# State-space scan on one core: transposed drive in blocks of 64 steps, B diagonals by state group, delta copied inside SBUF

## The reference

```
u: (B, K=4, D_INNER=192, L=4096)        four scan directions
x_dbl = einsum('bkdl,kcd->bkcl', u, x_proj_weight)
dts, Bs, Cs = split(x_dbl, [6, 6 + 16], axis=2)
delta = softplus(einsum('bkrl,kdr->bkdl', dts, dt_projs_weight) + dt_projs_bias)
A = -exp(A_logs)                        # (K, 192, 16)
for t in range(L):                      # h: (B, K, 192, 16)
    h = h * exp(delta_t[..., None] * A) + (delta_t * u_t)[..., None] * B_t[:, :, None, :]
    y_t = einsum('bkdn,bkn->bkd', h, C_t)
```

## Time and profile before

| what | us |
|---|---|
| median of 3 runs (16163.91 to 16176.15) | 16174.73 |
| the profiled execution, its own time | 16179.37 |
| span of that execution in the trace | 16176.9 |
| PE busy, share of the span | 12939.1, 80% |
| DVE busy | 9552.7, 59% |
| POOL busy | 8899.6, 55% |
| ACT busy | 7503.2, 46% |

### The profile page before, as it was taken

How to read it: one execution, slowest core, us unless ns; L and a number is a source line. 1 busy time by engine, 2 the same in 40 slices (tenths; PEclk the granted TensorE clock), 3 DMA queues, 4 the chain that set the end, 5 groups by cost and what they waited for, 6 DMA issues and landing times.

```text
span 16176.9 us, 551693 instructions
## 1 busy us (share of the span) xinstructions
PE 12939.1 (80%) x223648; PEld 6772.7 (42%) x223648; DVE 9552.7 (59%) x14966; ACT 7503.2 (46%) x14253; POOL 8899.6 (55%) x4341
## 2 busy tenths in 40 slices
PE   7888778887788877888778887788877888778887
PEld 3444434444344443444434444344443444434444
DVE  4666446664466644666446674466744667346673
ACT  4544344443444434445344453444534445344553
POOL 3666336663366633666346672466624667246672
PEclk9999699996899968999699996999969999699996
DMA  3444124441244412444124441344413444134441
GB/s 86 109 109 111 34 71 109 111 108 34 73 107 110 108 35 72 109 111 108 33 76 110 105 110 32 77 108 106 110 33 77 108 105 111 32 78 106 107 110 28
DMA packets 1044001, 1404.93 MB, mean 87 GB/s; under 512 B 461935, under 2 KB 463504, under 8 KB 1041148
## 3 DMA queue, kind: packets, MB, share of 16 engines
q1 hardware_dynamic: 1041660, 1369.95, 33.3%
HBM read 1235.32 MB, written 134.23 MB: 85 GB/s over the span
## 4 chain that ended last, share of the span: by engine, by line
PE 51%; issue 18%; DVE 16%; ACT 4%; DMA 4%; POOL 4%; DVEq 2%; SPq 1%; POOLq 1%; ACTq 0%
PE ps L856 21%; DVE arena L1144 14%; PE ps L886 7%; PE ps L794 5%; DMA delta_rows<-arena 2%; PE ps L819 2%; PE ps L961 2%; PE ps L960 2%; PE ps L820 2%; POOL arena L463 2%; PE ps L939 2%; ACT arena L650 1%; POOL arena L487 1%; ACT arena L590 1%; DMA arena<-delta_rows 1%
## 5 line engine op out<-in xcount | busy, mean ns | idle before, releaser
L487 POOL TENSOR_TENSOR arena<-arena 128x1024 f32<-128x1024 f32 x3072 | 7282.7, 2383 | 3990.2 <-ACT arena L632 3535.9
L1144 DVE TENSOR_TENSOR_SCAN arena<-arena,ps 128x256 f32<-128x256 f32 x12288 | 7950.2, 720 | 2128.5 <-ACT arena L650 987.6
L856 PE MATMUL ps<-arena 64*32 64x128 f32 x196608 | 6478.8, 407 | 2222.7 <-DVE arena L1144 1614.9
L856 PEld LDWEIGHTS ps<-arena 64*32 64x32 f32 x196608 | 3959.4, 120 | 5099.0 <-issue 4176.2
L650 ACT ACTIVATE arena<-arena,negA 128x512 f32<-128x512 f32 x6144 | 4054.0, 710 | 472.0 <-DMA arena<-delta_rows 298.1
L886 PE MATMUL ps<-arena,gather 128*32 128x512 f32 x12288 | 2092.6, 610 | 28.0 <-POOL arena L487 28.0
L632 ACT ACTIVATE arena<-arena 128x2 f32<-128x2 f32 x2688 | 523.7, 195 | 1723.7 <-DVE arena L1144 1723.6
L463 POOL TENSOR_TENSOR arena<-arena 128x512 f32<-128x512 f32 x512 | 662.8, 1295 | 1070.5 <-ACT arena L589 1070.5
L1109 DVE SCALAR_TENSOR_TENSOR ps<-ps,dtb,arena 128x512 f32<-128x512 f32 x512 | 382.3, 747 | 1456.8 <-ACT arena L590 1456.8
L599 ACT ACTIVATE arena<-ps 32x512 f32<-32x512 f32 x256 | 150.9, 590 | 1684.3 <-PE ps L820 1684.3
L507 POOL TENSOR_TENSOR arena<-arena 128x512 f32<-128x512 f32 (+1 forms) x128 | 159.7, 1268 | 1232.1 <-ACT arena L717 1232.1
(11 more groups left out here) (172 smaller groups left out, 8983.8 us busy)
## 6 DMA issues: line engine op xcount, KB each, us to landing
arena<-b_runs SPq DMA_DIRECT2D x1024, 512.0 KB, 6.3
arena<-delta_rows SPq DMA_DIRECT2D x3072, 128.0 KB, 4.6
arena<-c_rows SPq DMA_DIRECT2D x512, 512.0 KB
delta_rows<-arena SPq DMA_DIRECT2D x256, 256.0 KB, 6.7
delta_rows<-arena SPq DMA_DIRECT2D x256, 128.0 KB, 2.2
arena<-in_x SPq DMA_DIRECT2D x128, 192.0 KB, 3.2
b_runs<-arena SPq DMA_DIRECT2D x1024, 8.0 KB, 1.9
out_tokens<-arena SPq DMA_DIRECT2D x64, 192.0 KB, 2.2
```

Of the source, the lines that this page charges most:

```text
L487: pool.tensor_tensor(h, h, c_rep[s // NG], ALU.mult).then_inc(weighted, 1)
L856: mm = pe.matmul(to, du_t[ch.par][rows, k, g * CW:(g + 1) * CW], runs[rows, j, :, :], start=True, stop=True)
L1144: dve.tensor_tensor_scan(h_out[:, a, cols][:, flip], decay[s % RDA][:, a, cols][:, flip], ps[:, 2 * (s % 2) + half, a * HALF:(a + 1) * HAL ...
```

## The change

It does five things.

1. du is transposed in blocks of 64 consecutive steps instead of every fourth step (`steps` replaces `every`). The output of a fill matmul is then contiguous over the 64 steps. The transposes become plain matmuls with the identity, 8 instead of 4 for each of the three.
2. The diagonal of B is stored with the state group outermost, so that the moving operand of a fill has a stride of 2 elements. B's transpose goes to partitions 64 to 127 of bank 5 instead of bank 7. The diagonals are written straight to their places by 8 DMAs of 8-byte pieces, 4096 pieces for a chunk, instead of 4 DMAs of 32-byte pieces, 1024 of them.
3. Delta isn't written to DRAM. 24 copies inside SBUF, each 32 partitions x 2 KB, replace the 2 writes and the 12 loads. `t_l` has two buffers.
4. The high channels come first in `GROUPS`, so that a new chunk starts with what is ready first, and the delta of its first two steps is loaded ahead of C.
5. The steps of a chunk at which the next one is prepared are spread: `copy_bc` and `clamp_exp` 0 from step 1 to step 2 of ACT, there behind the decays instead of ahead of them, `at_least_log` 0 from step 2 to 5 of DVE, `make_delta` 0 from 3 to 6, those for v = 1 from 6 and 7 to 8, `save_du` 0 from 5 to 10 and `save_du` 1 from 10 to step 0 of the next chunk, the PE transposes from 1, 4, 9 to 2, 8, 10.

```diff
-        GROUPS = (0, 1, 2, 3, 4, 5, 2, 3, 0, 1, 4, 5)
-        def every(ap, k):
-            return ap.rearrange("p (t k) -> p t k", k=NB)[:, :, k]
+        GROUPS = (4, 5, 0, 1, 2, 3) * NPR
+        BT_ROWS = slice(DHI, P)
+        def steps(h, k):
+            return slice(h * HALF + k * TB, h * HALF + (k + 1) * TB)
...  prepare (SP)
-                    for pr in range(NPR):
-                        for h in range(2):
-                            runs = f_dram[par][pr][h * HALF * PITCH + SKEW:h * HALF * PITCH + SKEW + HALF * PITCH]
-                            sp.dma_start(runs.rearrange("(k t w) -> t k w", t=TB, w=PITCH)[:, :, 0:RUN],
-                                         b_t[h * TB:(h + 1) * TB, :, pr * RUN:(pr + 1) * RUN]).then_inc(b_written, 16)
-                    wait_apart(sp, delta_done, ch.n(2, 1))
...
-                    sp.dma_start(delta_dram[par][DLO:DI, :], t_l[ch.r0:ch.r0 + DHI, :]).then_inc(delta_written[0], 16)
+                    for h in range(2):
+                        for j in range(NJ):
+                            spots = bass.AP(f_dram[par].tensor, f_dram[par].offset + h * FLEN + j * 2 * TB, [[PITCH + 2, TB], [TB * PITCH, NPR * NB], [1, 2]])
+                            sp.dma_start(spots, b_t[BT_ROWS, h, :, 2 * j:2 * j + 2]).then_inc(b_written, 16)
...  load_delta (SP)
-                        for j in range(NJ):
-                            sp.dma_start(delta_rep[j * CW:(j + 1) * CW, 2 * i:2 * i + 2, :], rows).then_inc(delta_loaded[i], 16)
+                        wait_apart(sp, delta_done, ch.n(2, v + 1))
+                        r0 = 2 * CW * i if v else ch.r0
+                        for g in range(2):
+                            for j in range(NJ):
+                                sp.dma_start(delta_rep[j * CW:(j + 1) * CW, 2 * i + g, :], t_l[v][r0 + g * CW:r0 + (g + 1) * CW, :]).then_inc(delta_loaded[i], 16)
...
                     load_b(0)
+                    load_delta(2)
                     load_c(0)
-                    wait_apart(sp, delta_done, ch.n(2, 2))
-                    sp.dma_start(delta_dram[par][0:DLO, :], t_l).then_inc(delta_written[1], 16)
                     load_delta(0)
                     load_delta(1)
                     load_b(1)
-                    load_delta(2)
                     load_c(1)
...  body (ACT)
-                            if s == 1:
-                                copy_bc(nx)
-                                clamp_exp(nx, 0)
-                            if s == 2:
-                                save_bt(nx)
-                                square_log(nx, 0)
-                            if s == 4:
-                                clamp_exp(nx, 1)
-                            if s == 5:
-                                save_du(nx, 0)
-                                square_log(nx, 1)
-                            if s == 10:
-                                save_du(nx, 1)
+                        if nx and s == 10:
+                            save_du(nx, 0)
                         if s + 2 < NSTEP:
                             decays(ch, s + 2)
                         elif nx:
                             decays(nx, s + 2 - NSTEP)
+                        if s == 0 and not ch.first:
+                            save_du(ch, 1)
...  save_y moves from s == 3 to s == 4, here
+                            if s == 2:
+                                copy_bc(nx)
+                                clamp_exp(nx, 0)
+                            if s == 3:
+                                save_bt(nx)
+                            if s == 4:
+                                square_log(nx, 0)
+                            if s == 6:
+                                clamp_exp(nx, 1)
+                            if s == 7:
+                                square_log(nx, 1)
...  turn_b, turn_du (PE)
-                    for k in range(NB):
-                        mm = pe.transpose(bank(LO_BANK)[:, k * NS:(k + 1) * NS], every(bc_raw[r, :], k), ident[r, ch.d0:ch.d0 + NS])
+                    for h in range(2):
+                        for k in range(NB):
+                            to = bank(Y_BANK + 1)[BT_ROWS, h * NB * NS:(h + 1) * NB * NS].rearrange("p (q k n) -> p q k n", k=NB, n=RUN)[:, :, k, :]
+                            mm = pe.matmul(to, bc_raw[r, steps(h, k)], ident[r, ch.d0:ch.d0 + NS].rearrange("p (q n) -> p q n", n=RUN), start=True, stop=True)
...
-                        mm = pe.transpose(bank(HI_BANK + v)[:, k * w:(k + 1) * w], every(du[r, :], k), ident[r, r])
+                        for h in range(2):
+                            mm = pe.matmul(bank(HI_BANK + v)[h * TB:(h + 1) * TB, k * w:(k + 1) * w], du[r, steps(h, k)], ident[r, r], start=True, stop=True)
...  fill (PE)
-                    if s == 0:
-                        wait_apart(pe, dut_saved, ch.n(2, 2))
+                    if s in (0, 2):
+                        wait_apart(pe, dut_saved, ch.n(2, 1 + s // 2))
...
-                        runs = b_diag[pr][:, k, :].rearrange("p (t j a) -> p j a t", j=NJ, a=2)
+                        spots = b_diag[pr][:, k, :].rearrange("p (j t a) -> p j a t", j=NJ, a=2)
...
-                                to = ps[j * CW:(j + 1) * CW, 2 * (s % 2) + h, :].rearrange("p (a t k) -> p a t k", a=2, k=NB)[:, :, :, k]
-                                mm = pe.matmul(to, du_t[ch.par][rows, k, g * CW:(g + 1) * CW], runs[rows, j, :, :], start=True, stop=True)
+                                to = ps[j * CW:(j + 1) * CW, 2 * (s % 2) + h, :].rearrange("p (a k t) -> p a k t", a=2, k=NB)[:, :, k, :]
+                                mm = pe.matmul(to, du_t[ch.par][rows, k, g * CW:(g + 1) * CW], spots[rows, j, :, :], start=True, stop=True)
...  body (PE): turn_b 1 -> 2, turn_du 0 4 -> 8, turn_du 1 9 -> 10
...  body (POOL): softplus_part 0 2 -> 4, times_u 0 3 -> 6, softplus_part 1 5 -> 7 (ahead of the weighting), times_u 1 7 -> 8
...  body (DVE)
-                            if s in (2, 6):
-                                at_least_log(nx, s // 6)
-                            if s in (3, 7):
-                                make_delta(nx, s // 7)
+                            if s == 5:
+                                at_least_log(nx, 0)
+                            if s == 6:
+                                make_delta(nx, 0)
+                            if s == 8:
+                                at_least_log(nx, 1)
+                                make_delta(nx, 1)
```

More of the change, by code:

```diff
@@ L205, in build @@
         du_t = [cv(NB * DI).rearrange("p (k d) -> p k d", d=DI) for _ in range(2)]
-        t_e, t_q, t_l, du, bc_raw = (cv(T) for _ in range(5))
-        b_t = cv(NB * NS).rearrange("p (k n) -> p k n", n=NS)
+        t_e, t_q, du, bc_raw = (cv(T) for _ in range(4))
+        t_l = [cv(T) for _ in range(2)]
+        b_t = cv(2 * NB * NS).rearrange("p (h i n) -> p h i n", h=2, n=RUN)
         state = cv(NCOL)
@@ L211, in build @@
         zeros = arena[:, ARENA - FLEN // P:ARENA]
[L213 removed]
+        f_dram = [nc.dram_tensor("b_runs%d" % par, (2 * FLEN,), F32, kind="Internal").ap() for par in range(2)]
         c_dram = [nc.dram_tensor("c_rows%d" % par, (NS, T), F32, kind="Internal").ap() for par in range(2)]
[L215 removed]
         cv = Carve()
@@ L586, in square_log @@
                     if not (ch.first and v == 0):
-                        act.wait_ge(du_done, ch.n(2, v))
-                        act.wait_ge(delta_written[1 - v], ch.n(16, 16 * v))
+                        act.wait_ge(delta_done, ch.n(2, v))
                     act.activation(t_q[:, :], t_e[:, :], ACT.Square, scale=0.5 ** 0.5).then_inc(sq_done, 1)
-                    act.activation(t_l[:, :], t_e[:, :], ACT.Ln, bias=one[:, :]).then_inc(ln_done, 1)
+                    if not ch.first:
+                        act.wait_ge(du_done, ch.n(2, v - 1))
+                        for i in ((0, 1) if v else (2,)):
+                            act.wait_ge(delta_loaded[i], ch.n(32 * NJ, 0))
+                    act.activation(t_l[v], t_e[:, :], ACT.Ln, bias=one[:, :]).then_inc(ln_done, 1)
                 def copy_bc(ch):
@@ L682, in body @@
                             decays(nx, s + 2 - NSTEP)
+                        if s == 0 and not ch.first:
+                            save_du(ch, 1)
+                        if s == 4 and not ch.first:
+                            kk, c = (ch.kk, ch.c - 1) if kind else (ch.kk - 1, NCH - 1)
+                            save_y(Chunk(ch.b, kk, c))
+                        if nx:
+                            if s == 2:
[3 more added lines that the diff above has]
+                                save_bt(nx)
+                            if s == 4:
+                                square_log(nx, 0)
[3 more added lines that the diff above has]
+                                square_log(nx, 1)
                     if nx is None:
```

63 lines of the change are left out of this document (22 added, 41 removed).

## The result

| | before | after |
|---|---|---|
| median, us | 16,175.44 | 14,617.36 |
| all runs | 16,163.91 to 16,185.27 | 14,597.91 to 14,637.12 (4) |
| span of the profiled execution | 16,176.9 | 14,602.8 |

The ratio is 0.9037, 95% interval 0.9021 to 0.9053: 9.6% faster. The forecast was 13,860 with a range of 13,000 to 15,000. Direction and range hold, but 757 us of the forecast gain are missing, and the time lies 117 us outside the likeliest case's own range (13,000 to 14,500). What follows looks for those 757 us.

What follows compares the result with a forecast made beforehand. PE had the most work, 39.7 of 48.4 us a chunk, with waits filling the rest. After the change: DVE's 33.8 plus 3.7 stalls plus 1.9 loop, 39.4 a chunk over 256 chunks, hence 13,860 us, range 13,000 to 15,000.

Steps and rivals of the forecast that it cites:

- the likeliest case: Whole kernel: the forecast of 13,860 us itself, own range 13,000 to 14,500, chance 0.66.
- strides of 8 and 4 elements: PE's fill: its strided access explains 1.99 us against a sum's 1.00; without it 1.0 to 1.2, 1.2 taken.
- the 4.0 taken: PE's three transposes in a chunk: 4.0 us assumed after the change, between 1.95 and 7.2.
- 33.8 + 3.7 = 37.5: DVE in one chunk: 33.8 us of work plus 3.7 of stalls make 37.5, before the loop's cost.
- the 1.9 of the loop: Hardware loop passes: PE's late, cut first fill adds 1.9 us a chunk on average, not hidden by faster fills.
- the 3.7 of stalls: DVE's scans in one chunk: losses of 0.5, 0.4, 0.6, 2.0 and 0.2 us over the steps.
- landed by 37: SP's queue: low delta ready at 30 us into the chunk, issued by 34.5, landed by 37, wanted by ACT at 37.5.
- 0.9 late, absorbed: PE at step 0: a projection behind the fill makes the next fill 0.9 us late, at no cost to the scans.
- Fill stays at 1.99: Rival on PE's fill: length unchanged, PE is the bound, a chunk takes 44.7 us, kernel 15,230; chance 0.12.
- A transfer is late: Rival on SP's DMA queue: 4 us a chunk above forecast, kernel 14,880; chance 0.11.
- PE's clock: Rival: idle PE slows, needing 32.2 + 32x us a chunk; x = 0.25 gives 14,600; chances 0.07 partial, 0.03 over half the time.
- The reordering does all the work: Rival: the layout's gain is hidden, DVE and POOL at 33.8 bound; 35.0 us a chunk, 12,750; no separate chance.

Runs made afterwards that it cites:

- oldorder: Changed kernel with the steps of ACT, PE, POOL and DVE put back where they were, short fills kept: 15,691 us, ratio 0.9695.
- warm: Changed kernel plus two useless PE matmuls at the end of each of steps 7, 8 and 11: 14,430.6 us, ratio 0.8911.
- shortcopy: Changed kernel with each delta copy moving 128 of 512 columns, in all chunks but the first, every issue kept: 14,619.23 us, ratio 0.9048.
- movstride: Changed kernel with the fill's moving operand (B's diagonal) back at a stride of 8 elements, output still contiguous: 15,237.84 us, ratio 0.9409.
- deltadram: Changed kernel with delta again going through DRAM, by two writes and twelve loads, all else kept: 15,224.97 us, ratio 0.9399.

## Why the prediction was right, and where it missed

**The layout of a fill.** Right in size: 1.2 forecast, 1.12 to 1.14 measured at the full clock. The reason was half right. I had "strides of 8 and 4 elements" as one suspect; it is the 8 of the moving operand alone. The transposes came out cheaper than the 4.0 taken: B's 1.03 (803.48 to 804.51), du's 0.68 and about 1.02 (788.42 to 789.44), 2.7 in all.

**The order.** The claim that `at_least_log` waits no more is right (5.4 a chunk to nothing; `oldorder` brings 4.8 back each time). The step that failed is the sum "33.8 + 3.7 = 37.5". With the 1.9 of the loop it has 5.6 of waits for DVE; measured are 9.1. The term that was mis-sized is the 3.7 of stalls. Averaged over all chunks but the first of each image, where the sum is 8.8 (9.1 is the first image's), DVE idles 4.8 ahead of steps 2 to 4 (forecast 1.5), 2.2 ahead of steps 5 to 8 (2.0), and 1.8 ahead of the rest, nearly all of it at the chunk's edge (0.2). Three causes can be named, with what the runs show of each:
- The clock. I wanted it above 0.9 and got 0.85. The projection behind a pause costs 3.39 for 1.98, a fill at the chunk's end 1.89 for 1.14. `warm` shows 187 us of the 757. It doesn't lift the clock fully and its idle matmuls take PE's time, so I take this for a lower bound.
- Low delta. I had it "landed by 37" after the chunk's start, wanted at 37.5. In the chunk from 745.04 it is ready at 33.8 instead of 30, wanted at 41.8, and there at 46.4. The issue price (0.80, not 0.56) and the landing were too low. It holds ACT, `save_du(ch, 1)` behind it, and fill(2). But `shortcopy` shows that shortening this wait by 40% gains nothing: the idle time moves from steps 2 and 3 to steps 4 to 8. What taking all of it away would give wasn't tried.
- PE's burst. From fill(2) on, PE has two projections, B's transpose, the carry and four sums between eight fills. My walk let "0.9 late, absorbed" vanish in the reserve of two PSUM buffers. In the trace the lateness is handed on to steps 3 and 4: from 793.63 to 817.8 in the chunk shown PE works without a pause but for one hole of 0.58, 24.2 for eight steps that are 20.6 of scans and 1.4 of softplus for DVE. `shortcopy` supports this, since step 4 waits longest also where fill(2) is in time. But no run that moved a projection or the carry out of the burst was made, so how much of the remaining some 570 us it holds stays open. So does moving `save_du(ch, 1)` ahead of `decays(ch, 2)`.

**The loop.** Forecast 1.9 a chunk, unchanged. The trace has less: the chunk at a pass is 44.0 long beside a neighbour of 41.4, 2.6 more, where it was 7.7 more. Over the whole run the 64 chunks at a pass take 43.9 and the others 42.1, where before it was 55.3 and 46.5. So the loop costs some 0.4 a chunk (1.8 x 64 / 256). I had said that faster fills don't hide it; something in the change does, and no run tells what. In `warm` the chunks at a pass are 4.3 longer than the others again.

**SP's queue.** B's writes right (5.74 for 6.1), and in the stage no wait of PE is put down to B's diagonal. One bound was worked out wrongly: eight issues at 0.76 are 6.1 already if pieces don't matter, and not 3.0. The measured 0.72 apiece says that doubling the pieces of an issue costs nothing. The copy inside SBUF is worth 608 us, which my sum never priced by itself.

**The rivals.** "Fill stays at 1.99": refuted for this kernel, and `movstride` shows what it would have given: 15,238, forecast 15,230. "A transfer is late": it happens, 103.3 us of ACT's waits in the stage, 3.2 a chunk near the 4 named. By my own sign of being wrong, "if ACT or PE waits on delta", this part of the forecast failed; yet a third less of the wait changed the time by nothing, and only a larger one (`deltadram`) cost time. "PE's clock": happens with x = 0.30 and costs far less than the formula says, as far as `warm` shows. "The reordering does all the work": refuted, the short fill is worth 621 us in the new order.

That the time fell into the stated range is in part luck. With the loop's 0.4 left out the stalls were 8.4 a chunk and not 3.7, and 1.5 of these 4.7 was given back by a loop that cost 0.4 and not 1.9. Of the signs that I had named for being right, the length of the fill, the wait at `at_least_log` and the 45 at a pass (43.9) came; the scans in runs of more than 16, chunks of 37 to 38, PE under DVE in busy time (1091.69 against 1075.88) and a clock above 0.9 did not.

## What to carry to other kernels

Look at the stride in bytes with which PE reads SBUF, for the moving operand and for weights: at 32 bytes a fill took 1.99, at 8 bytes 1.12; with weights at 16 bytes B's transpose took 2.01, contiguous 1.03; the output's stride was free. When one engine's stall is removed and another's work shortened, undo each alone and both together: here 160 and 613 us alone were 1,234 together. A shorter wait in one place is no gain by itself: in `shortcopy` it came back two steps later, so look at the idle time of the engine that sets the time step by step, over many chunks. And a walk over steps has to carry lateness along: it is absorbed only if the producer pauses before the next step, not if it has more work than the average for five steps.

## What was not expected of the hardware

- The short fill takes 1.12 at the upper level of the clock and 1.89 at the lower (823.83, granted 0.50). The long one takes 1.99 in a stage granted 0.97 and 2.03 in a stretch granted 0.50 of `movstride` (1054.82 to 1056.85):

```profile
1054.82 2.10 PE L851 MATMUL ps<-arena 64*32 64x128 f32 x64
1056.85 1.28 PE L881 MATMUL ps<-arena,gather 128*32 128x512 f32 x8
```

  The clock hardly matters to a long fill, and at the lower level a short one is hardly shorter: the gain of the layout exists only while PE keeps its clock.
- A pause alone doesn't make the next fill slow: the fill behind a pause of 2.04 at 819.88 took 1.12, and the one behind the next pause, of 2.15 at 823.83, took 1.89.
- Six matmuls of no use in a chunk raised the granted clock from 0.85 to 0.94 and made the kernel 1.3% faster.
- An issue of a copy inside SBUF kept SP for 0.59 at the median whether its 32 pieces had 2048 or 512 bytes, but single ones took up to 2.1.
